# Softmax sums from TensorE and their inverse applied to the attention output, in a window-attention and graph-attention block

## What is computed

```python
xn = layernorm over channels(x)
q, k, v = windows of roll(Wq xn + bq), roll(Wkv xn + bkv)
attn = einsum('bhct,bhcs->bhts', q, k) * DK ** -0.5 + bias + mask
attn = softmax(attn, axis=-1)                  # over the 64 pixels s of a window
out  = einsum('bhts,bhcs->bhct', attn, v)
x1   = x + Wproj roll_back(out) + bproj
t    = layernorm over channels(x1)             # tokens
h    = t @ W_gat                               # node rows: h and two attention terms
alpha = softmax over the edges of a node(leaky_relu(a_src[src] + a_dst[dst]))
gates = softmax of the top 2 of layernorm(segment_sum(h[src] * alpha))
y    = x1 + sum_e gates_e * (gelu(t @ W1_e + b1_e) @ W2_e + b2_e)
```

## Time and profile before

| | |
|---|---|
| median of three runs | 8292.23 us |
| profiled execution | 8293.7 us, span 8291.6 us |
| busy in the span: PE, DVE, ACT, POOL | 35%, 47%, 23%, 57% |
| mean granted TensorE clock | 0.652 of full speed |

### The profile page before, as it was taken

The page is one execution under the profiler, slowest core; times in us unless marked ns, Lnnn a source line. Parts: engine busy times, 40 slices in busy tenths (PEclk is TensorE's granted clock), DMA queues, the critical chain, the costliest instruction groups (busy, mean ns, idle before and its releaser), DMA issues.

```text
span 8291.6 us, 47516 instructions
## 1 busy us (share of the span) xinstructions
PE 2933.2 (35%) x14234; PEld 1451.6 (18%) x14234; DVE 3906.0 (47%) x4181; ACT 1884.4 (23%) x2801; POOL 4730.4 (57%) x4876
## 2 busy tenths in 40 slices
PE   2556667666322221222222122221212212100578
PEld 2334444443200000101000010010000000000223
DVE  5998888888523332432333333231111211112799
ACT  1334545444212121211212122121111111100000
POOL 0111211111477777777777777777777777776641
PEclk8778888888665665656666566665656656555555
DMA  1000000000122222222222222221111111111455
GB/s 50 20 25 31 30 31 31 25 28 25 56 60 55 69 73 52 70 58 69 55 69 73 52 73 68 57 62 31 40 34 36 40 30 40 33 23 23 144 184 175
DMA packets 284779, 455.28 MB, mean 55 GB/s; under 512 B 121214, under 2 KB 204382, under 8 KB 262366
## 3 DMA queue, kind: packets, MB, share of 16 engines
q1 hardware_dynamic: 134760, 395.02, 13.1%
q0 software_dynamic: 147648, 56.99, 7.0%
q10 hardware_dynamic: 2208, 1.05, 0.0%
HBM read 231.29 MB, written 221.42 MB: 55 GB/s over the span
## 4 chain that ended last, share of the span: by engine, by line
POOL 50%; issue 19%; DVE 3%; PE 1%; DMA 1%; POOLq 0%; ACT 0%; DVEq 0%
POOL gath L1308 49%; PE bank L1550 1%; DVE yo L1523 1%; POOL got L1585 1%; DMA gate_rows<-gate_dram 0%; DMA gate_dram<-turned_gates 0%; DVE fin L1528 0%; DVE s L1484 0%; DVE sc L1459 0%; POOL first L1737 0%; DVE s L1457 0%; DVE sc L1471 0%; DVE sc L1463 0%; DVE sc L1469 0%; DVE sc L1478 0%
## 5 line engine op out<-in xcount | busy, mean ns | idle before, releaser
L1308 POOL DMA_INDIRECT gath<-node_rows,idx x4352 | 4129.0, 949 | 1326.1 <-issue 1326.1
L1261 PE MATMUL bank<-xm,w_s 128*128 128x512 f32 x1024 | 642.3, 772 | 3751.2 <-ACT scratch_i L1282 3738.6
L1217 DVE TENSOR_TENSOR adst_in<-bank,gath 128x256 f32<-128x256 f32 x68 | 53.4, 786 | 2823.9 <-DMA gath<-node_rows,idx 2823.9
L1261 PEld LDWEIGHTS bank<-xm,w_s 128*128 128x128 f32 x1024 | 227.1, 241 | 4150.0 <-ACT scratch_i L1282 4005.7
L1289 ACT ACTIVATE bank<-diff 128x256 f32<-128x256 f32 x68 | 26.3, 387 | 3742.9 <-DVE diff L1234 3742.9
L1035 POOL TENSOR_TENSOR scratch_i<-xc,dst_f 128x480 f32<-128x480 f32 x64 | 86.3, 1348 | 1302.3 <-ACT dst_f L952 1302.3
L1204 DVE TENSOR_SCALAR scratch_i<-bank,b_s 128x512 f32<-128x512 f32 x256 | 190.2, 749 | 916.5 <-PE bank L1268 523.0
L1268 PE MATMUL bank<-scratch_i,w_s 128*128 128x512 f32 x1024 | 539.1, 683 | 193.0 <-ACT scratch_i L1282 116.3
L1550 PE MATMUL bank<-gate_rows,choose 4*128 4x512 f32 x512 | 447.4, 1064 | 60.1 <-DVE yo L1523 50.1
L1282 ACT ACTIVATE scratch_i<-bank,b_s 128x512 f32<-128x512 f32 x512 | 345.3, 683 | 187.8 <-PE bank L1261 187.1
L1585 POOL DMA_INDIRECT got<-edge_rows,end_i x256 | 245.6, 959 | 206.3 <-DVE gates L1511 128.7
(11 more groups left out here) (215 smaller groups left out, 5879.6 us busy)
## 6 DMA issues: line engine op xcount, KB each, us to landing
gath<-node_rows,idx POOLq DMA_INDIRECT x4352
y_dram<-scratch_i SPq DMA_DIRECT2D x64, 1024.0 KB, 4.0
yo<-y_dram SPq DMA_DIRECT2D x64, 1024.0 KB, 5.2
edge_rows<-rows SPq DMA_DIRECT2D x68, 768.0 KB, 3.4
line<-moved SPq DMA_DIRECT2D x21, 2048.0 KB, 7.0
moved<-line SPq DMA_DIRECT2D x20, 2048.0 KB
scratch_i<-in_x SPq DMA_DIRECT2D x64, 256.0 KB, 2.7
x_dram<-x SPq DMA_DIRECT2D x64, 256.0 KB, 2.2
```

The costliest lines, as they stand in the source:

```text
L1261: e.matmul(bank[:, k % 2, :], w1_s[:, k // 2, P * (k % 2):P * (k % 2) + P], xm[par][:, :], start=True, stop=True).then_inc(up_full, 1)
L1308: e.indirect_dma_start(gath[par][:, j, :], None, node_rows, bass.IndirectOffsetOnAxis(ap=idx[par][:, j:j + 1].bitcast(U32), axis=0)).then_ ...
```

## The change

The probabilities are no longer divided by their row sums. PE makes the sums from the transposed exponentials: four matmuls per half round with a constant 0/1 matrix `heads` (a 64-column half of it as the stationary operand, `pt` as the moving one, 512 columns), placed in `attend` before the last two windows' value matmuls, into bank 4. Every output channel then holds its head's sum. ACT takes the logarithm and exp(-log) of that bank into `inv[g]` (`inverse_sums`, behind `copy_transposed(g)`), and DVE multiplies the attention output by it as it leaves PSUM (`weigh_attention`, in place of ACT's `copy_attention`). `inverse_sum` is gone from DVE; `attend` waits for `exp_ready` instead of `probs_ready`. The counts of `pt_full[0]` and `pt_evac[0]` go from 4 to 6 per round. DVE's order becomes: weigh(0), scores(0), slot 0, weigh(1), slot 1, x1, scores(1), slot 2, node rows, slot 3. The weights of the sort slots stay.

```diff
-            def inverse_sum(g):
...
-                e.wait_ge(exp_ready, t * 2 + g + 1 + OPEN)
-                own.step(e.tensor_reduce(row_sum[:, g], prob[g][:, :, :, :], AX, ALU.add))
-                own.settle()
-                own.step(e.reciprocal(row_inv[:, g], row_sum[:, g]))
-                own.settle()
-                pr = prob[g][:, :, :, :].rearrange("p w h s -> p (w h) s")
-                e.tensor_tensor(pr, pr, row_inv[:, g].rearrange("p w h -> p (w h)").unsqueeze(2)
-                                .broadcast_to([P, 32, L]), ALU.mult).then_inc(probs_ready, 1)
-
+            def weigh_attention(g, u):
+                if not has_c:
                     return
+
+                wait_full(e, t, u)
+                e.wait_ge(sums_turned, t * 2 + g + 1 + OPEN)
+                e.tensor_tensor(ot[:, 8 * g:8 * g + 8].rearrange("p w i j -> p (w i j)"), bank[:, 6 + u % 2, :],
+                                inv[g][:, :], ALU.mult).then_inc(evac[u % 2], 1)
+
+            weigh_attention(0, 0)
             scores(0)
             if t:
                 sort_slot(d, t, 0)
-            inverse_sum(0)
+            weigh_attention(1, 3)
+            sort_slot(d, t, 1)
             if has_c:
...
-            sort_slot(d, t, 1)
             scores(1)
             sort_slot(d, t, 2)
...
-            inverse_sum(1)
             sort_slot(d, t, 3)
...
-                e.wait_ge(probs_ready, t * 2 + g - 1 + OPEN)
+                e.wait_ge(exp_ready, t * 2 + g - 1 + OPEN)
...
+                    if wp == 4:
+
+                        heads = con("heads").rearrange("p (v c) -> p v c", v=2)
+                        e.wait_ge(pt_evac[0], pt_uses(t, g, 0) + 2 + OPEN)
+                        for hh in range(2):
+                            for v in range(2):
+                                m = e.matmul(bank[64 * hh:64 * hh + 64, 4, :], heads[:, v, :],
+                                             pt[:, :, hh, 64 * v:64 * v + 64], start=v == 0, stop=v == 1)
+                        m.then_inc(pt_full[0], 1)
...
-            def copy_attention(g, u):
+            def inverse_sums(g):
                 if not has_c:
                     return
-                wait_full(e, t, u)
-                e.activation(ot[:, 8 * g:8 * g + 8], bank[:, 6 + u % 2, :].rearrange(
-                    "p (w i j) -> p w i j", i=WS, j=WS), ACT.Copy).then_inc(evac[u % 2], 1)
+
+                e.wait_ge(pt_full[0], pt_uses(t, g, 0) + 3 + OPEN)
+                e.activation(inv[g][:, :], bank[:, 4, :], ACT.Ln).then_inc(pt_evac[0], 1)
+                e.wait_ge(pt_evac[0], pt_uses(t, g, 0) + 3 + OPEN)
+                e.activation(inv[g][:, :], inv[g][:, :], ACT.Exp, scale=-1.0).then_inc(sums_turned, 1)
...
             copy_transposed(0)
-            copy_attention(0, 0)
+            inverse_sums(0)
...
             copy_transposed(1)
+            inverse_sums(1)
             exponentials(0)
-            copy_attention(1, 3)
```

More of the change, by code:

```diff
@@ L45 @@
                   ("pair_even", 1), ("pair_odd", 1),
-                  ("sign", 9), ("next_base", 256), ("shift_mask", 4 * L), ("row_base", 2), ("earlier", 16)):
+                  ("sign", 9), ("next_base", 256), ("shift_mask", 4 * L), ("row_base", 2), ("earlier", 16),
+                  ("heads", P)):
     CONST[_name] = (_at, _at + _n)
@@ L84, in constants @@
     put("row_base", np.stack([p * EC - 1, EDGES + p * TC - 1], 1))
+    k, v, d = np.arange(P) // L, np.arange(2), np.arange(4 * DK) // DK
+    put("heads", (2 * k[:, None, None] + v[None, :, None] == d[None, None, :]).reshape(P, P))
     put("earlier", (np.arange(NE)[None, :] < np.arange(NE)[:, None]).reshape(1, NE * NE))
@@ L216, in program @@
         exp_ready = sem("exp_ready")
-        probs_ready = sem("probs_ready")
+        sums_turned = sem("sums_turned")
         pt_full = [sem(f"pt_full{b}") for b in range(2)]
@@ L325, in program @@
         row_max = sb("row_max", [P, 2, 8, NH // 2])
-        row_sum = sb("row_sum", [P, 2, 8, NH // 2])
-        row_inv = sb("row_inv", [P, 2, 8, NH // 2])
+        inv = [sb(f"inv{g}", [C, 8 * L]) for g in range(2)]
         ot = sb("ot", [C, NWIN, WS, WS])
@@ L612, in scores @@
                 e.wait_ge(s_full, t * 2 + g + 1 + OPEN)
-                e.wait_ge(pt_full[1], t * 4 + 2 * g + 2 + OPEN)
+                e.wait_ge(pt_full[1], pt_uses(t, g, 1) + 2 + OPEN)
                 kind = 2 * ((t - 1) % 16 // 15)
@@ L683, in round_dve, with pt_uses @@
                 pass_over(e, node_done, t * 2, 2)
-            inverse_sum(1)
             sort_slot(d, t, 3)
+        def pt_uses(t, g, b):
+            each = 3 - b
+            return t * (2 * each) + each * g
         def wait_evac(e, t, u):
@@ L716, in turn_eighth @@
             if k < 2:
-                e.wait_ge(pt_evac[k], t * 4 + 4 + OPEN)
+                e.wait_ge(pt_evac[k], t * (6 - 2 * k) + 6 - 2 * k + OPEN)
             else:
@@ L728, in turn_tail_pe @@
             e.wait_ge(turn_asked, 2 * LEVELS + 1 + OPEN)
-            e.wait_ge(pt_evac[0], t * 4 + 4 + OPEN)
+            e.wait_ge(pt_evac[0], t * 6 + 6 + OPEN)
             for b in range(2):
@@ L762, in attend @@
                 if not has_c:
-                    for b in range(2):
-                        pass_over(e, pt_full[b], t * 4 + 2 * g, 2)
-                        pass_over(e, pt_evac[b], t * 4 + 2 * g, 2)
+                    for b, each in ((0, 3), (1, 2)):
+                        pass_over(e, pt_full[b], t * 2 * each + each * g, each)
+                        pass_over(e, pt_evac[b], t * 2 * each + each * g, each)
+                    pass_over(e, sums_turned, t * 2 + g, 1)
                     skip(u)
                     return
-                e.wait_ge(probs_ready, t * 2 + g - 1 + OPEN)
+                e.wait_ge(exp_ready, t * 2 + g - 1 + OPEN)
                 for wp in range(5):
@@ L773, in attend @@
                     if wp < 4:
-                        e.wait_ge(pt_evac[b], t * 4 + 2 * g + wp // 2 + OPEN)
+                        e.wait_ge(pt_evac[b], pt_uses(t, g, b) + wp // 2 + OPEN)
                         for w in range(2):
@@ L784, in attend @@
                         free(u)
-                    e.wait_ge(pt_evac[(wp - 1) % 2], t * 4 + 2 * g + (wp - 1) // 2 + 1 + OPEN)
+                    e.wait_ge(pt_evac[(wp - 1) % 2], pt_uses(t, g, (wp - 1) % 2) + (wp - 1) // 2 + 1 + OPEN)
+                    if wp == 4:
[6 more added lines that the diff above has]
+                        m.then_inc(pt_full[0], 1)
                     for w in (2 * wp - 2, 2 * wp - 1):
@@ L922, in copy_transposed @@
                     b = wp % 2
[L923 removed]
+                    e.wait_ge(pt_full[b], pt_uses(t, g, b) + wp // 2 + 1 + OPEN)
                     e.activation(pt[:, 2 * wp:2 * wp + 2], bank[:, 4 + b, :].rearrange(
                         "p (w h t) -> p w h t", w=2, h=2), ACT.Copy).then_inc(pt_evac[b], 1)
[L927 removed]
+            def inverse_sums(g):
                 if not has_c:
                     return
[L930 to L932 removed]
+                e.wait_ge(pt_full[0], pt_uses(t, g, 0) + 3 + OPEN)
+                e.activation(inv[g][:, :], bank[:, 4, :], ACT.Ln).then_inc(pt_evac[0], 1)
+                e.wait_ge(pt_evac[0], pt_uses(t, g, 0) + 3 + OPEN)
+                e.activation(inv[g][:, :], inv[g][:, :], ACT.Exp, scale=-1.0).then_inc(sums_turned, 1)
             def centered_copy(n, u0):
@@ L1591, in _ @@
         def _(e):
-            for t in (biased, centered, probs_ready, chunk_step, diff_ready, edge_used, *y_evac, gate_step, gates_ready, fin_ready,
+            for t in (biased, centered, chunk_step, diff_ready, edge_used, *y_evac, gate_step, gates_ready, fin_ready,
                       gate_asks, gate_asks2, turn_asked, node_done, weighed):
@@ L1675, in _ @@
         def _(e):
-            for t in (idx_ready, *evac, exp_ready, *pt_evac, rstd_ready, turned_copy, hidden, weights_ready, rows_done,
+            for t in (sums_turned, idx_ready, *evac, exp_ready, *pt_evac, rstd_ready, turned_copy, hidden, weights_ready, rows_done,
                       gate_std, gate_exp):
```

2 lines of the change are left out of this document (removed).

## The result

The changed kernel takes 8098.2 us (median of four runs, 8095.9 to 8098.5) against 8292.1 us before on the same chip: a ratio of 0.9765, 95% interval 0.9749 to 0.9782, or 194 us less. The forecast was 8080 us with a range of 8045 to 8150. The profiled execution took 8098.4 us with a span of 8096.5; its mean granted clock is 0.661.

A forecast was written before the change was run, and what follows sets the result against it. DVE was taken to bound the first stage (attention and sort), with the gathers following one for one. Savings of 61, 62, 49, 41 and -0.4 us total 213, from 8293.7 to 8080 us, range 8045 to 8150.

The forecast's parts named there:

- the tail: Round 33, at the end of the first stage: nothing covers the two attentions, so 0.4 us is lost.
- out-turn rounds: Rounds 8, 11, ..., 29, where DVE waits for the node copy: 49 us saved over the eight.
- one for one: Time taken off attention and sort moves POOL's gathers, the rest of the run, forward unchanged by the same amount.
- The first rival: PE's sums run one after another, 3.2 to 3.6 us per half: 8111 to 8125 us, chance 0.25.
- Full rounds: Rounds 10, 13, ..., 31, DVE busy nearly throughout: each falls to 46.8 us, 7.8 saved, 62 over eight.
- W1: DVE's second new product per round, ahead of means and projections: no wait in rounds 10, 13, ..., 31.
- W0: DVE's first new product per round, ahead of scores(0); it waits for attend(0), its sums and `inv`.
- Rounds 1 to 7: Early rounds, DVE alone sets the pace: 9.9 us saved in round 1, then 8.5 each, 61 together.
- the second rival: PE keeps the upper clock through attend(0), 6.0 us instead of 7.7, saving 25 more: 8055 us, chance 0.13.
- Back-turn rounds: Rounds 9, 12, ..., 30, node copy set by the centring of x1: 41 us saved over the eight.
- both at once with the lower clock: Third rival: PE's sums one after another and at the lower clock, 7.5 us per half: 8310 us, chance 0.04.
- the second stage: POOL's gathers after the sort; a fourth rival has their DMA or gathers take the gain back: 8292 us, chance 0.03.

The follow-up runs named there:

- experiment 4: Kernel after with POOL's product for x2 made on only 16 of 512 columns, the rest zero (wrong results): 8056.4 us, ratio 0.9708.
- experiment 5: Kernel before with POOL's product for x2 made on only 16 of 512 columns, the rest zero: 8267.4 us, ratio 0.9962.
- experiment 1: Kernel after with sort slot 1 put back behind the x1 additions, as in the kernel before: 8171.7 us, ratio 0.9847.
- experiment 3: Kernel after with the sums at full width, 128-column zero-padded weights in one accumulation group: 8152.8 us, ratio 0.9823.

## Why the prediction was right, and what it missed

The forecast took 213 us off the stage, and 195 came off. What bounds the kernel, the prices and the effect of the order were right. The miss is the lengthened exchanges (some 20 us), which the sum held fixed, and the tail (4.5); against them stand idle times in the out-turn rounds that grew by 10 us less than forecast.

**What bounds it, and one for one:** right. The stage lost 194.7 us, and the rest did not move beyond its spread.

**The prices.** The sums were taken at 2.2 us a half and took 1.94 in 63 of 64 half rounds (granted clock 1.00 over those at 1054.91); that is the lower end of the bounds (1.9 for halves fully beside each other), and the row of L790 had pointed to it. The first rival's reckoning, in which only one instruction of the second half overlaps the first half, would have made it 3.2 us; here the eight instructions (two for each of the four matmuls) took 1.94, and 3.70 only at full width, so the reckoning fell. In the trace of the sums above they start in pairs, a pair every 0.43 to 0.48 us. Which two make a pair the records do not tell. The new product was taken at 0.65 us and costs 0.685 in the mean. `inv` follows 0.6 + 0.6 us behind the sums, as summed, and ACT loads no table in the stage but the one at 1.77 us (1.28 us long): the next is at 1975.11, behind the first gather's start.

**Full rounds:** 46.8 forecast, 47.4 to 48.1 measured. W1 doesn't wait there and scores(0) wait 0.4, as said. The step that failed is "DVE's work is 54.6 - 2 x 4.32": it lets every remaining pass keep its length. The eight full rounds fell 6 us short, and their exchanges grew by 7.4: they take 15.9 us more in the kernel after than in experiment 4, and 8.5 more in the kernel before than in experiment 5. Without the collision in either kernel only 3.4 of the 6 come back (59.2 in the table), as W0 then waits for `inv` behind some of these rounds, up to 2.32 us in experiment 4.

**Rounds 1 to 7** fell short by 10, and rounds 3 and 4 carry 7.8 of it: they saved 4.7 and 4.6 us where 8.5 were forecast. Their exchanges take 3.9 and 4.1 us more than before. About half of that is x2's product, which met no exchange in these two rounds before. The other half stays in experiment 4 (40.9 us of exchanges in each of the two rounds, against 39.0 in experiment 5) and goes with POOL's first product (L1050), which both experiments left alone. In round 4 of the kernel after it lies beside slot 1; DVE's timeline, then POOL's:

```profile
372.70 2.22 DVE L422 TENSOR_TENSOR key_a<-key_b 128x1024 f32<-128x1024 f32 x1
...
377.26 2.21 DVE L421 TENSOR_TENSOR key_b<-key_a 128x1024 f32<-128x1024 f32 x1
```

```profile
372.21 1.63 POOL L1050 TENSOR_TENSOR scratch_i<-xc,dst_f 128x480 f32<-128x480 f32 x1 [35.34 <-ACT dst_f L967]
...
376.23 2.17 POOL L1050 TENSOR_TENSOR scratch_i<-xc,dst_f 128x480 f32<-128x480 f32 x1
```

Two passes of 1.22 take 2.2 us. That the first product is the cause here is read from the timeline and was not tried. In rounds 2, 5, 6 and 7 the exchanges are 1 us shorter than before, and scores(1) wait about 1 us for PE, which the forecast did not have; these two cancel.

**Out-turn rounds** came out at 49.4 against 49, but by two errors that cancel, and that is luck. Their exchanges were lengthened by 8.2 us more than before. Against that, the forecast added some 20 us of idle time to DVE in these rounds (8 x 8.64 of work taken off, 49 saved), and the trace shows 9.7. In round 14 this is PE's clock. The forecast had PE at the lower level in attend(0) behind every such round, from one row (1.97 us at 1032.32, granted clock 0.50); in the kernel before the way from the first transpose to the scores takes 7.62 us behind rounds 8 and 14 only, and 5.25 to 6.71 behind the other six. PE's timeline of the kernel after, behind out-turn rounds 14 and 17:

```profile
950.99 1.09 PE L781 MATMUL bank<-cst,prob 128*128 128x128 f32 x8 [0.71 <-DVE node L671]
...
957.96 2.06 PE L817 MATMUL bank<-k,q 64*128 64x128 f32 x32
```

```profile
1104.54 1.96 PE L781 MATMUL bank<-cst,prob 128*128 128x128 f32 x8 [0.72 <-DVE node L671]
...
1113.87 2.06 PE L817 MATMUL bank<-k,q 64*128 64x128 f32 x32
```

From the first transpose to the scores it is 6.97 us in the one (granted clock 1.00 throughout) and 9.33 in the other (0.67 in the mean, 0.50 in the transposes at 1104.54): the second rival's mechanism, in some rounds. Round 14 took 54.99 us where 56.6 was forecast, round 17 56.58. Over all eight the way is 2.0 us longer than before in the mean, which is the price of the sums, so on the whole the clock gave nothing back in this kernel. In experiment 4 seven of the eight took 6.98 and the one behind round 20 took 8.40, which goes with its 64.6 us in the table. How much of that is the clock and how much the earlier x2 was not separated, and why the other rounds waited less than forecast stays open.

**Back-turn rounds** came out 3 us better than forecast (51.1 in round 15, as said). The **tail** was mis-sized: nothing covers the last two attentions, and DVE waits for `inv` in full, twice, where before it waited once for the projection (9.51 us). The new product, DVE's timeline after:

```profile
1931.99 0.69 DVE L643 TENSOR_TENSOR ot<-bank,inv 128x512 f32<-128x512 f32 x1 [8.80 <-ACT inv L947]
1942.27 0.69 DVE L643 TENSOR_TENSOR ot<-bank,inv 128x512 f32<-128x512 f32 x1 [9.58 <-ACT inv L947]
```

That costs 4.9 us instead of 0.4.

**The rivals.** Sums in file are real and cost what was said when forced, but are not what this kernel does; both at once with the lower clock did not occur, as the sums take 1.94 us in 63 of the 64 half rounds and 2.22 in the other; the second stage took nothing back that its spread would show.

## What to carry to other kernels

When an operation is removed from a busy engine, ask also what ran beside it on the other engines, for free: here the move slid POOL's products from beside a reduction to beside two-buffer passes, and some 20 us, a tenth of the gain, went that way without any wait showing in the trace; only the mean durations of unchanged instructions tell it (2571 ns against 2305 for the exchange's first pass from `key_b` to `key_a`). Moving the small product to the engine that it was delaying was cheaper here than leaving it beside that engine's passes (8070.4 us against 8099.8). Where a new step's latency lies on the path, a reordering that puts queued work over it (here slot 1 over the projection, 66 us) can be worth as much as the work removed.

## What the runs showed of the hardware

In the rows of the kernels before and after and of experiment 1, a DVE pass over two SBUF buffers (2048 columns, 2.28 us) took 3.24 to 3.36 us where a POOL product of 512 columns that reads SBUF was issued during the pass before it and that pass, too, read two buffers; beside products of 16 columns, in the rows of experiment 4, it took 2.28 to 2.30. The two POOL products at 1037.91 in the kernel after take 2.24 and 3.31 us, where the shortest in that trace takes 1.26. A reduction beside such a product, in round 13 of the kernel before, keeps its 2.29 us. Eight fp32 instructions of 512 columns take 1.94 us in two 64-column halves (kernel after) and 3.70 us at full width (experiment 3), both at a granted clock of 1.00.
